# The second normalisation written wholly by GpSimd, with VectorE's part in it taken away

## The chip, the core and the metric

The kernel runs on one core of a Trainium2 chip. A core has TensorE (PE, with its weight loads as PEld), VectorE (DVE), ScalarE (ACT), GpSimd (POOL) and SyncE (SP), each with its own instruction queue, and they meet only through semaphores. The metric is the device time of one launch in microseconds, lower is better.

## What is computed

Sixteen blocks of 128 tokens with 128 features go through gated cross-attention and then through a mixture of nine experts, two chosen per token:

```python
x = x + tanh(g_xattn) * xattn(ctx, layernorm(x), mask, mask, ...)     # 8 heads of 16
x = x + tanh(g_ffn) * ffn(layernorm(x), ...)                          # this layernorm is the second normalisation

def _layernorm(x, axis=-1, eps=1e-05):
    return (x - mean) / sqrt(var + eps)

# ffn: scores = sigmoid(x @ gate.T + bias); top 2 of 9 experts, weights scaled to sum 1
#      out += cw[:, e] * ((silu(x @ w1[e].T) * (x @ w3[e].T)) @ w2[e].T)
```

All arithmetic is float32 except where the experts' first products are split into two float32r parts.

## The kernel before

There are three stages. **Projections**: keys, values, queries and the first half of the output projection, four groups of four blocks. **Attention and routing**: a software pipeline over steps k = 0 to 16 (`turns(step)` on every engine). In step k, PE makes the scores of block k, turns the probabilities of block k-1 and multiplies them with the values, and finishes block k-2 (turn, normalise, output projection). Block k-3 gets its second normalisation: its normalised rows are turned by PE (line 1039) and multiplied with the gate weights (line 1047). **Experts**: token rows that were scattered into a table in DRAM by expert are read back in 40 tiles of 128 rows, go through one expert each, and are scattered to a second table; the last blocks of the attention stage are finished between the first tiles (`between(k)` on each engine). At the end the two results per token are added.

Every engine works through its program in the order written; what sets the order is the code itself, and nothing reorders it. PE's order within a step is: scores, turn of block k-2, turn of the probabilities, `turn_rows` (line 1033 for block k-2, then line 1039 for block k-3, which waits for semaphore `ln2`), the products with the values (line 1001), `gate_and_out` (lines 1047, 1049). So line 1001 stands behind line 1039 in the queue.

The second normalisation of block b, in step b+3: DVE adds the block to x (line 745) and takes mean and variance into `mv2` (lines 747, 751, semaphore `var2`). POOL adds epsilon (line 496) and raises to the power -0.5 (line 498, into `rs2`, semaphore `rstd2`). DVE writes (x - mean) * rs2 into copy 0 of `stage` (line 725, semaphore `ln2`). POOL copies copy 0 to copy 1 (line 490, `keep`, semaphore `kept`), because every token row goes to two experts. POOL then scatters both copies of a group's blocks by indirect DMA (line 508), one group of four blocks some steps later: two of these DMAs in steps 9 and 13, two in steps 10 and 14, four in steps 11 and 15. POOL also prepares the values of each block (lines 475, 477). DVE's order in a step is: maxima of the first four heads (line 706), `unturn` (lines 712, 716), line 725, maxima of the last four heads (line 706), routing work that differs from step to step, and line 745 onwards.

The last two blocks, 14 and 15, are normalised at the start of the expert stage: line 725 for them stands in DVE's `between(0)` and `between(2)`, and PE turns the rows in its own `between(0)` and `between(2)`. POOL does lines 496 and 498 for them among the scatters of group 2, ahead of its first expert tile.

Of the kernel before, what the change touches and what calls it, by code (L numbers as in the profile page):

```python
# [18 lines left out]
ALU = mybir.AluOpType  # L19
# [7 lines left out]
P = 128  # L27
NB = 16
D = 128
# [3 lines left out]
UN = 4  # L33
# [29 lines left out]
def build(nc, x, ctxT, mask, maskT, g2, consts, w_srcT, b_src, w_tgtT, b_tgt, w_outT, b_out,  # L63
          w13T, w2T, gateT, gate_b, x_rows, y_rows, out):
    with ExitStack() as ctx:
# [29 lines left out]
        xs = sb("xs", [P, NB, D])  # L95
# [28 lines left out]
        stage = sb("stage", [P, 2, 2, UN, RW])  # L124
# [80 lines left out]
        def on(k, lag):  # L205

            return 0 <= k - lag < NB
# [224 lines left out]
        def _(pool):  # L432
# [37 lines left out]
            def step(k, r, i):  # L470
# [7 lines left out]
                if on(k, 3):  # L478
                    rstd2_of(k - 3)
# [3 lines left out]
                if on(k, 3):  # L483
                    keep(k - 3)

            def keep(b):

                par, place = b // UN % 2, b % UN
                pool.wait_ge(ln2, b + 1)
                nc.gpsimd.tensor_copy(stage[:, par, 1, place, 0:D], stage[:, par, 0, place, 0:D]).then_inc(kept, 1)  # L490

            def rstd2_of(b):

                q = b % 2
                pool.wait_ge(var2, b + 1)
                nc.gpsimd.tensor_scalar(ve2[:, q:q + 1], mv2[:, q, 1:2], LN_EPS, None, ALU.add).then_inc(eps_added, 1)
                pool.wait_ge(eps_added, b + 1)
                nc.gpsimd.tensor_tensor(rs2[:, q:q + 1], ve2[:, q:q + 1], minus_half[:, 0:1], ALU.pow).then_inc(rstd2, 1)

# [27 lines left out]
            rstd2_of(NB - 2)  # L527
            scatter(NG - 2, 0)
            keep(NB - 2)
            scatter(NG - 2, 1)  # L530
            rstd2_of(NB - 1)
            scatter(NG - 2, 2)
            keep(NB - 1)
# [8 lines left out]
        def _(dve):  # L542
# [176 lines left out]
            def norm2(b):  # L719

                q, par, place = b % 2, b // UN % 2, b % UN
                dve.wait_ge(rstd2, b + 1)
                if b >= 2 * UN:
                    dve.wait_ge(st_rows[place], (b // UN - 1) * 32)
                nc.vector.scalar_tensor_tensor(stage[:, par, 0, place, 0:D], xs[:, b, :], mv2[:, q, 0:1], rs2[:, q:q + 1].to_broadcast([P, D]),
                                               ALU.subtract, ALU.mult).then_inc(ln2, 1)

# [25 lines left out]
            def step(k, r, i):  # L753
# [4 lines left out]
                if on(k, 3):  # L758
                    norm2(k - 3)
# [116 lines left out]
            def between(k):  # L876

                if k == 0:
                    norm2(NB - 2)
                    table_used(0)  # L880
# [3 lines left out]
                if k == 2:  # L884
                    norm2(NB - 1)
                    table_rows(1)
# [318 lines left out]
```

## Time and profile before

| | us |
|---|---|
| median of 3 runs | 243.07 |
| the 3 runs | 243.07, 243.14, 240.57 |
| the profiled execution | 240.22 |
| its span in the trace | 238.4 |
| PE busy | 191.4 (80% of the span) |
| DVE, ACT, POOL busy | 145.1, 143.4, 127.7 |

The profiled execution is a run of its own: its time is 1.8 us above its span, and it lies 2.85 us under the median. The granted TensorE clock was 0.933 of full speed over that execution. Busy shares are means over three stages with different limits, so the stage matters more than the share.

### The profile page before, as it was taken

The page shows a single profiled execution, that of the slowest core. Times are in us where ns is not written, and L with a number is a line of the kernel's source. Part 1 is how long each engine was busy: PE and PEld are TensorE (multiplying, and loading weights), DVE is VectorE, ACT ScalarE, POOL GpSimd, SP SyncE. Part 2 cuts the span into 40 slices and gives each one's busy share as a digit, 9 for nine tenths or more (in the row PEclk, how much of TensorE's full clock was granted, in tenths as well). Part 3 has the DMA queues.
Part 4 walks back from the last instruction along what each step waited for, and adds up shares of the span by engine and source line. Part 5 has one row for each costly group of instructions (what it writes and reads, how often), then busy time and mean ns, then how long its engine had stood idle before and what let it go on. Part 6 is the DMA issues. An engine that isn't in the chain of part 4 may idle for free.

```text
span 238.4 us, 5685 instructions
## 1 busy us (share of the span) xinstructions
PE 191.4 (80%) x1480; PEld 157.7 (66%) x1481; DVE 145.1 (61%) x535; ACT 143.4 (60%) x401; POOL 127.7 (54%) x224
## 2 busy tenths in 40 slices
PE   0099898799997997898677969997999999998200
PEld 0087675457665664666456959997999999998100
DVE  1228788688799779799759447943343344442045
ACT  1525776998796887489433474765666666665100
POOL 4225644524552688468568533678776555555400
PEclk9999999999999999799857788999999999999955
DMA  4994999999900001001122111222321222110087
GB/s 144 344 293 114 311 364 405 404 404 341 303 20 1 26 22 45 3 22 37 36 73 78 48 36 43 76 67 68 94 82 51 61 53 59 44 39 27 0 301 227
DMA packets 21143, 30.78 MB, mean 129 GB/s; under 512 B 3312, under 2 KB 14324, under 8 KB 21120
## 3 DMA queue, kind: packets, MB, share of 16 engines
q1 hardware_dynamic: 17280, 25.74, 32.7%
q0 software_dynamic: 2304, 4.24, 5.4%
q10 hardware_dynamic: 1536, 0.54, 0.9%
q8 instruction: 10, 0.16, 0.3%
q14 instruction: 13, 0.11, 0.1%
HBM read 14.97 MB, written 16.05 MB: 130 GB/s over the span
## 4 chain that ended last, share of the span: by engine, by line
PE 52%; DVE 14%; DMA 11%; issue 7%; POOL 7%; ACT 6%; SPq 2%; POOLq 0%; DVEq 0%; ACTq 0%
PE pt_ps L1117 9%; DMA mask_b<-in_mask 6%; PE score_ps L1084 5%; POOL x_rows L508 4%; PE pt_ps L1126 4%; PE score_ps L1086 4%; PE score_ps L1085 4%; PE score_ps L951 4%; PE score_ps L927 3%; PE ps_a L1001 3%; DMA kheads<-y_rows 3%; DVE less L706 2%; PE score_ps L937 2%; PE pt_ps L989 2%; ACT probs L343 2%
## 5 line engine op out<-in xcount | busy, mean ns | idle before, releaser
L524 POOL DMA_INDIRECT y_rows<-probsT,ids x40 | 39.7, 992 | 26.6 <-ACT probsT L410 21.6
L343 ACT ACTIVATE probs<-score_ps,less 128x128 f32<-128x128 f32 x128 | 37.9, 421 | 0.4 <-DVE less L706 0.4
L508 POOL DMA_INDIRECT x_rows<-stage,slot x32 | 32.4, 1012 | 9.0 <-issue 8.0
L1117 PE MATMUL pt_ps<-w,probsT 128*128 x240 | 34.8, 283 | 1.4 <-ACT probsT L417 1.4
L1117 PEld LDWEIGHTS pt_ps<-w,probsT 128*128 128x128 f32 x240 | 32.7, 197 | 2.2 <-issue 1.9
L860 DVE TENSOR_TENSOR xg_low<-ps_a,xg_high 128x128 fp32r<-128x128 f32 x40 | 11.6, 290 | 34.8 <-ACT xg_high L395 34.6
L410 ACT ACTIVATE probsT<-pt_ps,xg 128x128 f32<-128x128 f32 x40 | 14.7, 367 | 29.7 <-PE pt_ps L1117 29.7
L1084 PE MATMUL score_ps<-w_high,xg_low 128*128 x80 | 30.8, 386 | 0.6 <-issue 0.2
L1086 PE MATMUL score_ps<-w_high,xg_high 128*128 x80 | 26.9, 336 | 0.0
L1085 PE MATMUL score_ps<-w_low,xg_high 128*128 x80 | 26.9, 336 | 0.0
L867 DVE TENSOR_TENSOR probs<-probs,score_ps 128x352 f32<-128x352 f32 x40 | 20.8, 520 | 9.8 <-ACT probs L402 9.0
L706 DVE TENSOR_REDUCE less<-score_ps 128x4 f32<-128x512 f32 x32 | 21.7, 684 | 4.9 <-PE score_ps L958 4.9
L402 ACT ACTIVATE probs<-score_ps 128x352 f32<-128x352 f32 x40 | 18.6, 466 | 4.7 <-PE score_ps L1086 4.2
L1126 PE MATMUL pt_ps<-cst,probs 128*128 128x128 f32 x120 | 20.4, 281 | 0.0
L927 PE MATMUL score_ps<-w_src,ctx_r 128*128 128x128 f32 x64 | 9.7, 314 | 13.2 <-DMA mask_b<-in_mask 13.2
L417 ACT COPY probsT<-pt_ps 128x384 f32<-128x384 f32 x40 | 19.1, 479 | 1.3 <-PE pt_ps L1126 1.3
L951 PE MATMUL score_ps<-kheads,qT 64*128 64x256 f32 x128 | 19.1, 419 | 0.1
L989 PE MATMUL pt_ps<-cst,probs 128*128 128x128 f32 x128 | 16.9, 274 | 1.6 <-ACT probs L343 1.6
L927 PEld LDWEIGHTS score_ps<-w_src,ctx_r 128*128 128x128 f32 x64 | 9.0, 225 | 13.3 <-issue 12.9
L1084 PEld LDWEIGHTS score_ps<-w_high,xg_low 128*128 128x128 f32 x80 | 16.0, 201 | 2.5 <-issue 1.7
L1085 PEld LDWEIGHTS score_ps<-w_low,xg_high 128*128 128x128 f32 x80 | 16.1, 202 | 0.0
L989 PEld LDWEIGHTS pt_ps<-cst,probs 128*128 128x128 f32 x128 | 14.4, 141 | 2.4 <-ACT probs L343 2.3
(150 smaller groups left out, 408.0 us busy)
## 6 DMA issues: line engine op xcount, KB each, us to landing
x_rows<-pads SPq DMA_DIRECT2D x1, 9945.0 KB, 35.4
w_low<-in_w13T SPq DMA_DIRECT2D x3, 1056.0 KB, 8.9
xg<-x_rows SPq DMA_DIRECT2D x40, 65.0 KB, 1.9
ctx_r<-in_ctxT SPq DMA_DIRECT2D x4, 512.0 KB, 6.2
w<-in_w2T SPq DMA_DIRECT2D x1, 1728.0 KB, 12.2
kheads<-y_rows SPq DMA_DIRECT2D x3, 512.0 KB, 5.0
mask_b<-in_mask SPq DMA_DIRECT2D x4, 256.0 KB, 7.3
xs<-in_x SPq DMA_DIRECT2D x3, 256.0 KB, 9.2
```

The lines of the kernel that those rows point to most:

```text
L343: last = nc.scalar.activation(probs[:, r % 2, h, :], score_ps[:, r % 2, h, :], ACT.Exp, bias=less[:, r % 2, h:h + 1])
L508: pool.indirect_dma_start(x_rows[:, :], bass.IndirectOffsetOnAxis(ap=slot[:, par, c, p:p + 1], axis=0), stage[:, par, c, p, :], None, boun ...
L524: pool.indirect_dma_start(y_rows[:, :], bass.IndirectOffsetOnAxis(ap=ids[:, r:r + 1], axis=0), yt[:, r, :], None, bounds_check=last_row, o ...
L706: nc.vector.tensor_reduce(less[:, r % 2, here], score_ps[:, r % 2, here, :], AX.X, ALU.max, negate=True).then_inc(lessened, 1)
L927: last = nc.tensor.matmul(bank[0][:, b * P:(b + 1) * P], ctx_r[:, r, f, b * P:(b + 1) * P], w_src[:, f, D:2 * D], start=(f == 0), stop=(f ...
L951: nc.tensor.matmul(score_ps[:, r % 2, half * HH + 2 * pair:half * HH + 2 * pair + 2, :], qT[rows, k * P:(k + 1) * P], kheads[rows, heads, ...
L989: last = nc.tensor.transpose(pt_ps[:, half, h, :], probs[:, q, half * UN + h, :], ident)
L1084: nc.tensor.matmul(dst[:, 0:HID], xg_low[:, q, :], of(w13_high), start=True, stop=False)
L1085: nc.tensor.matmul(dst[:, 0:HID], xg_high[:, q, :], of(w13_low), start=False, stop=False)
L1086: return nc.tensor.matmul(dst[:, 0:HID], xg_high[:, q, :], of(w13_high), start=False, stop=True)
L1117: last = nc.tensor.matmul(bank[5][:, 0:D], hidT[:, q3, c, :], w2[:, bass.ds(e3, 1), c, :].rearrange("p o d -> p (o d)"), start=(c == 0), s ...
L1126: last = nc.tensor.transpose(bank[4][:, c * P:(c + 1) * P], hid[:, q2, c0:c0 + P], ident)
```

## The change

POOL's `norm2` now does the whole second normalisation: epsilon, power, and then the row (x - mean) * rs2 written twice straight from x into copies 0 and 1 of `stage`, by two `tensor_scalar` instructions with the mean and the power as scalars per partition. The first signals `ln2`, the second `kept`. DVE's line 725 and POOL's copy (line 490) are gone. POOL now waits for its own `rstd2`, and the wait for the scatter that last read the place in `stage` (`st_rows`) moves from DVE to POOL. On POOL both rows are written ahead of the step's scatters; the copy stood behind them.

```diff
--- before.py
+++ after.py
@@ -476,26 +476,23 @@
                                             mask_t[:, bass.ds(k, 1)].unsqueeze(1).to_broadcast([P, H, HD]), ALU.mult)
                     nc.gpsimd.tensor_copy(v_cur[:, r, :, HD:HD + 1], live_t[:, bass.ds(k, 1)].unsqueeze(1).to_broadcast([P, H, 1])).then_inc(v_set, 1)
                 if on(k, 3):
-                    rstd2_of(k - 3)
+                    norm2(k - 3)
                 for p in range(UN):
                     if routed(k, r, 2 * UN + 1 + min(p, 2)) is not None:
                         scatter(routed(k, r, 2 * UN + 1 + min(p, 2)), p)
-                if on(k, 3):
-                    keep(k - 3)
-
-            def keep(b):
-
-                par, place = b // UN % 2, b % UN
-                pool.wait_ge(ln2, b + 1)
-                nc.gpsimd.tensor_copy(stage[:, par, 1, place, 0:D], stage[:, par, 0, place, 0:D]).then_inc(kept, 1)
-
-            def rstd2_of(b):
-
-                q = b % 2
+
+            def norm2(b):
+
+                q, par, place = b % 2, b // UN % 2, b % UN
                 pool.wait_ge(var2, b + 1)
                 nc.gpsimd.tensor_scalar(ve2[:, q:q + 1], mv2[:, q, 1:2], LN_EPS, None, ALU.add).then_inc(eps_added, 1)
                 pool.wait_ge(eps_added, b + 1)
                 nc.gpsimd.tensor_tensor(rs2[:, q:q + 1], ve2[:, q:q + 1], minus_half[:, 0:1], ALU.pow).then_inc(rstd2, 1)
+                pool.wait_ge(rstd2, b + 1)
+                if b >= 2 * UN:
+                    pool.wait_ge(st_rows[place], (b // UN - 1) * 32)
+                for c, done in enumerate((ln2, kept)):
+                    nc.gpsimd.tensor_scalar(stage[:, par, c, place, 0:D], xs[:, b, :], mv2[:, q, 0:1], rs2[:, q:q + 1], ALU.subtract, ALU.mult).then_inc(done, 1)
 
             def scatter(g, p):
 
@@ -524,13 +521,11 @@
                 pool.indirect_dma_start(y_rows[:, :], bass.IndirectOffsetOnAxis(ap=ids[:, r:r + 1], axis=0), yt[:, r, :], None,
                                         bounds_check=last_row, oob_is_err=False).then_inc(st_y[r], 16)
 
-            rstd2_of(NB - 2)
+            norm2(NB - 2)
             scatter(NG - 2, 0)
-            keep(NB - 2)
             scatter(NG - 2, 1)
-            rstd2_of(NB - 1)
+            norm2(NB - 1)
             scatter(NG - 2, 2)
-            keep(NB - 1)
             scatter(NG - 2, 3)
             for k in range(NT):
                 tile(k, k % TR)
@@ -716,15 +711,6 @@
                 nc.vector.tensor_tensor(upd[:, q, :].rearrange("p (h d) -> p h d", h=H), turned[:, :, 0:HD],
                                         rden[:, q, :].unsqueeze(2).to_broadcast([P, H, HD]), ALU.mult).then_inc(normed, 1)
 
-            def norm2(b):
-
-                q, par, place = b % 2, b // UN % 2, b % UN
-                dve.wait_ge(rstd2, b + 1)
-                if b >= 2 * UN:
-                    dve.wait_ge(st_rows[place], (b // UN - 1) * 32)
-                nc.vector.scalar_tensor_tensor(stage[:, par, 0, place, 0:D], xs[:, b, :], mv2[:, q, 0:1], rs2[:, q:q + 1].to_broadcast([P, D]),
-                                               ALU.subtract, ALU.mult).then_inc(ln2, 1)
-
             def logits_of(g):
 
                 dve.wait_ge(lg_mm, g * UN + UN)
@@ -755,8 +741,6 @@
                     maxima(k, r, 0)
                 if on(k, 2):
                     unturn(k - 2, r % 2)
-                if on(k, 3):
-                    norm2(k - 3)
                 if on(k, 0):
                     maxima(k, r, 1)
                 if 2 + k < NE:
@@ -876,13 +860,11 @@
             def between(k):
 
                 if k == 0:
-                    norm2(NB - 2)
                     table_used(0)
                 if k == 1:
                     second(NB - 1)
                     table_counts(1)
                 if k == 2:
-                    norm2(NB - 1)
                     table_rows(1)
                 if k == 3:
                     logits_of(NG - 1)
```

In the order of POOL's instructions, in steps 9 and 10 (`stage` holds the normalised rows, `v_cur` the values of one block, `rs` is the power, `ve` the variance with epsilon), there stood before:

```order
L496 TENSOR_SCALAR ve<-mv 128x1
L498 TENSOR_TENSOR rs<-ve,minus_half 128x1
L508 DMA x_rows<-stage,slot 19712x130 x2
L490 COPY stage<-stage 128x128
L475 TENSOR_TENSOR v_cur<-vals,mask_t 128x8x16
L477 COPY v_cur<-live_t 128x8
L496 TENSOR_SCALAR ve<-mv 128x1
L498 TENSOR_TENSOR rs<-ve,minus_half 128x1
```

And now, in the same steps:

```order
L488 TENSOR_SCALAR ve<-mv 128x1
L490 TENSOR_TENSOR rs<-ve,minus_half 128x1
L495 TENSOR_SCALAR stage<-xs,mv,rs 128x128 x2
L505 DMA x_rows<-stage,slot 19712x130 x2
L475 TENSOR_TENSOR v_cur<-vals,mask_t 128x8x16
L477 COPY v_cur<-live_t 128x8
L488 TENSOR_SCALAR ve<-mv 128x1
L490 TENSOR_TENSOR rs<-ve,minus_half 128x1
```

One instruction behind the scatters has become two ahead of them. In the order of DVE's instructions, in step 13 (`upd` is the attention's output, `less` the negated maxima, `filled` the first instruction of a table for the experts), there stood before:

```order
L706 TENSOR_REDUCE less<-score_ps 128x4
L712 RECIPROCAL rden<-ps_b 128x8
L716 TENSOR_TENSOR upd<-ps_b,rden 128x128
L725 SCALAR_TENSOR_TENSOR stage<-xs,mv,rs 128x128
L706 TENSOR_REDUCE less<-score_ps 128x4
L806 TENSOR_TENSOR filled<-next_row,cst 1x144
```

And now, in the same step:

```order
L701 TENSOR_REDUCE less<-score_ps 128x4
L707 RECIPROCAL rden<-ps_b 128x8
L711 TENSOR_TENSOR upd<-ps_b,rden 128x128
L701 TENSOR_REDUCE less<-score_ps 128x4
L790 TENSOR_TENSOR filled<-next_row,cst 1x144
```

DVE goes from `upd` straight to the second maxima. PE's, ACT's and SP's instructions are the same in both kernels, in the same order.

## Rows read from the trace of the kernel before

**Rows 1.** The page: the chain that ended last, shares of the span by engine
```profile
PE 52%; DVE 14%; DMA 11%; issue 7%; POOL 7%; ACT 6%; SPq 2%; POOLq 0%; DVEq 0%; ACTq 0%
```

**Rows 2.** Stretches: length, busy PE, PEld, DVE, ACT, POOL; PE clock; DMA share; GB/s
```profile
44.00:68.00 24.00, 23.07 (x231) 15.47 (x231) 17.93 (x45) 21.40 (x71) 10.14 (x23) 1.00 0.92 326
68.00:98.00 30.00, 25.65 (x266) 18.01 (x262) 25.53 (x111) 22.36 (x74) 17.86 (x38) 0.99 0.06 20
```

**Rows 3.** Groups by line: busy us, mean ns; then idle before
```profile
L475 POOL TENSOR_TENSOR v_cur<-vals,mask_t 128x128 f32<-128x128 f32 x16 | 7.2, 450 | 0.0
L490 POOL COPY stage<-stage 128x128 f32<-128x128 f32 x16 | 4.8, 302 | 7.5 <-DVE stage L725 7.5
L725 DVE SCALAR_TENSOR_TENSOR stage<-xs,mv,rs 128x128 f32<-128x128 f32 x16 | 5.5, 344 | 0.4 <-POOL rs L498 0.4
```

**Rows 4.** Timeline of DVE in step 11: start us, us, instruction
```profile
89.31 0.34 DVE L725 SCALAR_TENSOR_TENSOR stage<-xs,mv,rs 128x128 f32<-128x128 f32 x1
89.57 0.68 DVE L706 TENSOR_REDUCE less<-score_ps 128x4 f32<-128x512 f32 x1
```

**Rows 5.** Timeline of POOL, steps 9 to 12
```profile
79.04 0.57 POOL L498 TENSOR_TENSOR rs<-ve,minus_half 128x1 f32<-128x1 f32 x1
79.94 1.23 POOL L508 DMA_INDIRECT x_rows<-stage,slot  x1 [0.33 <-DVE slot L700]
...
83.54 0.23 POOL L496 TENSOR_SCALAR ve<-mv 128x1 f32<-128x1 f32 x1 [0.30 <-DVE mv L751]
...
87.95 0.24 POOL L496 TENSOR_SCALAR ve<-mv 128x1 f32<-128x1 f32 x1 [0.16 <-DVE mv L751]
88.27 0.57 POOL L498 TENSOR_TENSOR rs<-ve,minus_half 128x1 f32<-128x1 f32 x1
89.03 1.10 POOL L508 DMA_INDIRECT x_rows<-stage,slot  x1 [0.19 <-issue]
...
93.95 0.30 POOL L490 COPY stage<-stage 128x128 f32<-128x128 f32 x1
94.21 0.41 POOL L475 TENSOR_TENSOR v_cur<-vals,mask_t 128x128 f32<-128x128 f32 x1
...
95.08 0.57 POOL L498 TENSOR_TENSOR rs<-ve,minus_half 128x1 f32<-128x1 f32 x1
```

**Rows 6.** Timeline of PE in step 12
```profile
96.36 0.27 PE L1039 MATMUL ps_b<-cst,stage 128*128 128x128 f32 x1
```

**Rows 7.** The chain that ended last, steps 13 to 16: start us, us, what
```profile
101.83 0.34 DVE stage L725
...
105.66 0.57 POOL rs L498
...
116.25 0.58 POOL rs L498
...
116.85 0.36 DVE stage L725
...
117.26 0.33 PE ps_b L1039
```

**Rows 8.** Timeline, blocks 14 and 15 at the start of the experts
```profile
121.01 0.57 POOL L498 TENSOR_TENSOR rs<-ve,minus_half 128x1 f32<-128x1 f32 x1
121.89 1.11 POOL L508 DMA_INDIRECT x_rows<-stage,slot  x1 [0.31 <-DVE slot L700]
...
127.03 0.25 POOL L496 TENSOR_SCALAR ve<-mv 128x1 f32<-128x1 f32 x1
127.36 0.57 POOL L498 TENSOR_TENSOR rs<-ve,minus_half 128x1 f32<-128x1 f32 x1
129.45 0.33 PE L1039 MATMUL ps_b<-cst,stage 128*128 128x128 f32 x1 [1.09 <-DVE stage L725]
```

**Rows 9.** POOL's line 477 in step 3, and DVE beside it
```profile
53.29 0.86 POOL L477 COPY v_cur<-live_t 128x8 f32<-128x8 f32 x1
53.15 0.94 DVE L583 TENSOR_TENSOR w_low<-w_low,w_high 128x704 fp32r<-128x704 f32 x1
```

## The prediction

> **What bounds the kernel now.** I first read the chain that ended last, for who sets the end: PE 52%, DVE 14%, POOL 7% [rows 1]. Then the busy time by stretch, because the change only touches the attention steps and the first expert tiles. From 44 to 68 us (steps 2 to 6, no scatters) ACT is busy 21.40 of 24.00 us and POOL 10.14: these steps are ACT's and PE's, and POOL has room. From 68 to 98 us (steps 7 to 11) DVE is busy 25.53 of 30.00 and POOL 17.86, the scatters having begun [rows 2]. Last I read the timelines of POOL and PE, for how much room stands between the end of POOL's power and the moment PE turns the rows. The reader is to see three things. After a power in a late step POOL goes straight on: at 88.84 it ends, and the scatter starts at 89.03 [rows 5]. Late in step 11's four scatters POOL is behind: the power of block 9 ends at 95.65, PE's line 1039 starts at 96.36, and PE has line 1001 queued behind it [rows 5, 6]. And in steps 14 to 16 the chain itself runs through POOL: power at 105.66, scatters from 106.42, power at 116.25, DVE's line 725 at 116.85, PE at 117.26 [rows 7].
>
> **What DVE loses.** Sixteen instructions of 0.344 us [rows 3]. Line 725 starts at 89.31 and the next at 89.57, so each holds the queue for 0.26 us [rows 4], 16 x 0.26 = 4.2 us in all. In the ACT-bound steps, blocks 0 to 3, that is worth nothing: ACT's work hides it, and if ACT were faster it would be worth at most 0.26 us a step. It is on the path where DVE ends the step: step 7 (block 4), step 11 (block 8) and step 13 (block 10, on the chain at 101.83 [rows 7]). Step 11's gain is spent again, because step 12 waits for POOL; I count steps 7 and 13, **-0.26 x 2 = -0.52 us**.
>
> **What POOL gets.** It loses the copy, 0.302 us long [rows 3], from 93.95 to the next start at 94.21, so 0.26 of the queue [rows 5]. It gets two instructions that read 128x128, subtract a scalar and multiply by another. No row shows this form; call its duration d. The lower end is the copy of the same size, 0.30. The upper end is two passes with two operands each, as line 475 is (0.41 at 94.21 [rows 5]): 0.76 when the second follows within 0.05 of the first's end. I take **d = 0.40**: one streamed operand like the copy, but two scalars to fetch and two operations, so close to line 475 and its mean of 0.45 [rows 3]. A pair costs more than 2d by little: POOL waits for its own power, which costs 0.08 (the epsilon ends at 88.19, the power starts at 88.27 [rows 5]), and the second overlaps the first by 0.05. So each pair puts 2d + 0.03 = 0.83 us ahead of the step's scatters and takes 0.26 away behind them. PE's wait changes too: it was power, DVE's line, PE; it is power, 0.08, d, and 0.05 to signal PE.
>
> The Trainium skill bears on d. By its page GPSIMD Engine Reference (section 4.1, Engine selection) elementwise work with two inputs is about twice as slow on GpSimd, with one input roughly line-rate, and the page advises VectorE for it. Twice line 725 would be about 0.69; the trace here has a one-input copy at 0.302, under DVE's 0.344, which speaks for the one-input half of that rule. By the two-input half the sum below would be about +5.4 instead of +1.1.
>
> **Steps 9 to 12.** The first scatter could start at 79.04 + 0.57 + 0.19 = 79.80 and starts at 79.94, for the slots: 0.14 of room [rows 5]. Three pairs go ahead of scatters (blocks 6, 7, 8), three copies go. POOL idled 0.30 before the epsilon at 83.54 and 0.16 before the one at 87.95 [rows 5]; this room is filled first. So the power of block 9 ends 3 x 0.83 - 3 x 0.26 - 0.14 - 0.46 = 1.11 later than 95.65. PE then starts line 1039 at 96.76 + 0.08 + 0.40 + 0.05 = 97.29 instead of 96.36: **+0.93 us**, in d it is 7d - 1.87. Line 1001, the value products and the next scores stand behind it, so all of it counts.
>
> **Steps 14 to 16.** POOL has no idle left once `var2` of block 11 has come. Pairs for blocks 11 and 12, less two copies: 2 x 0.57 = 1.14. For block 13 the power ended at 116.83 and PE started at 117.26, 0.43 later [rows 7]; now 0.53. That is 1.14 + 0.10 = **+1.24 us**, or 5d - 0.76. The same POOL delay moves the scatters of group 1; their readers, the first expert tiles, start after 120 us and have that room.
>
> **Blocks 14 and 15, among the tiles.** The scatter at 121.89 had 0.12 of room behind a power that ended at 121.58 (0.19 of the 0.31 being the usual gap) [rows 8]. Pair in, copy out: epsilon and power of block 15 come 0.83 - 0.12 - 0.26 = 0.45 later, so the power ends at 128.38. But DVE's line 725 stood behind an expert tile's multiply there, and PE waited until 129.45, 1.09 of it idle [rows 8]. Now PE can start at 128.38 + 0.53 = 128.91: **-0.54 us**, 3d - 1.74. If d were small this gain would end at the 1.09.
>
> What else moves costs nothing: steps 3 to 8 have no scatter beside POOL's pairs, and POOL's 10.14 of 24 us leaves the room [rows 2]; the wait for `st_rows` that POOL takes over looks at scatters issued at least two steps earlier on the same queue; group 2's scatters end about 1 us later, ahead of tiles that PE reaches only some ten us afterwards, where POOL waits for the tiles anyway.
>
> **The sum**: -0.52 + 0.93 + 1.24 - 0.54 = **+1.1 us**, in d it is 15d - 4.9. Its ends are -0.4 (d = 0.30) and +6.5 (d = 0.76). Against the profiled execution's 240.22 that is 241.3. The median lies 2.85 above that execution, and two of three runs lie at 243.1, so I forecast the median at 243.07 + 1.1 = **244.2 us**.
>
> **The rivals.**
> 1. *The rows are dear on POOL.* Same mechanism, other side of the bound: 1% is 2.4 us (about what a measurement of this kernel can tell from no change, its own runs lying 1.1% apart), and 15d - 4.9 reaches it at d = 0.49. At 0.55 the time is 243.07 + 3.3 = 246.4. For it: scalars from memory, and 0.23 to 0.25 for an epsilon of one element per partition, which a copy of 128 undercuts per element by far [rows 5, 8]. Against it: the copy's 0.302 [rows 3]. Chance 0.27.
> 2. *POOL and DVE block each other over memory reads.* The 8-element copy at 53.29 took 0.86 us beside DVE's long two-operand line 583 from 53.15 [rows 9]. POOL now reads 32 x 128 elements where it read 16. If each pair of the ten blocks 6 to 15 met one such block of 0.2 us (an estimate between nothing and the 0.86), that is another +2.0, 246.2 in all. Against it: line 583 ends with step 6, and DVE's line 725, itself a reader of two operands from that memory, is gone; the instructions that now stand there read PSUM. By the Trainium skill, SBUF — State Buffer (section Who interferes with whom), a DVE instruction with two SBUF inputs and a GpSimd one that reads SBUF exclude each other; the row at 53.29 agrees, with 0.86. A falling TensorE clock, as PE waits longer in steps 12 and 16, works the same way. Chance 0.14.
> 3. *The relief of DVE decides.* If POOL's lag were covered, as it would be were the steps DVE's throughout, the 16 x 0.26 = 4.2 us would be gained: 238.9. Against it: ACT's 21.40 of 24.00 in five steps [rows 2], and the chain on POOL after 105 us. Chance 0.08.
>
> That the change does not do what it says is excluded by the order of instructions. My forecast's own mechanism, with d between 0.30 and 0.49, has 0.51. Faster by over 1%: 0.08; within 1%: 0.51; slower: 0.27 + 0.14 = 0.41. The range: low, the forecast's low end of -0.4 and up to 1.7 less, because the median may fall toward the lower of the runs shown, 241.0; high, d = 0.60 with +4.1, 247.2.
>
> **What would show it.** In the changed kernel, the two new POOL instructions at 0.40 each (0.30 to 0.49), with starts 0.35 apart. DVE's second maxima starting right behind `upd`. PE's line 1039 of step 12 waiting for POOL by about 1 us more than before, and the chain going from POOL's rows straight to PE in step 16. The gap before line 1039 in the tiles (1.09) smaller by half. It is wrong if the new form costs over 0.5, if DVE's instructions get longer beside it, if the mean granted clock moves far from 0.933, or if PE's wait in steps 12 and 16 does not grow.

## The result: 4% slower, and outside the range

The changed kernel takes 251.01 us (median of 4 runs, 246.95 to 254.05) against 241.82 for the kernel before (4 runs, 239.09 to 243.14). The ratio is 1.040, with a 95% interval of 1.027 to 1.053. The forecast was 244.2, range 241.0 to 247.2, with "within 1%" likelier than "slower". The direction was the forecast's, the size was not. Where a ratio with an interval is given, here and below, it compares only each kernel's faster runs, since most of the others show a lower granted clock; medians are over all runs. The profiled execution took 250.45 us with a span of 248.6, against 240.22 and 238.4 before.

The page of the changed kernel, first the shares of the chain that ended last and then the group of the new instruction (busy us, mean ns, idle before it):

```profile
PE 43%; POOL 22%; DMA 10%; DVE 9%; issue 8%; ACT 5%; SPq 2%; POOLq 0%; DVEq 0%; ACTq 0%
L495 POOL TENSOR_SCALAR stage<-xs,mv,rs 128x128 f32<-128x128 f32 x32 | 25.5, 801 | 1.7
```

POOL's share of the chain went from 7% [rows 1] to 22%. The new instruction takes 0.801 us, where the sum had 0.40 and its upper bound 0.76.

POOL's timeline in the steps of [rows 5] (L490 is now the power, L488 the epsilon, L505 the scatter; x2 is the pair of rows):

```profile
79.77 0.57 POOL L490 TENSOR_TENSOR rs<-ve,minus_half 128x1 f32<-128x1 f32 x1
80.44 1.58 POOL L495 TENSOR_SCALAR stage<-xs,mv,rs 128x128 f32<-128x128 f32 x2
82.22 1.23 POOL L505 DMA_INDIRECT x_rows<-stage,slot  x1 [0.20 <-issue]
...
90.95 0.25 POOL L488 TENSOR_SCALAR ve<-mv 128x1 f32<-128x1 f32 x1
91.29 0.57 POOL L490 TENSOR_TENSOR rs<-ve,minus_half 128x1 f32<-128x1 f32 x1
91.97 1.61 POOL L495 TENSOR_SCALAR stage<-xs,mv,rs 128x128 f32<-128x128 f32 x2
93.75 1.10 POOL L505 DMA_INDIRECT x_rows<-stage,slot  x1 [0.18 <-POOL stage L495]
...
99.54 0.57 POOL L490 TENSOR_TENSOR rs<-ve,minus_half 128x1 f32<-128x1 f32 x1
100.22 1.59 POOL L495 TENSOR_SCALAR stage<-xs,mv,rs 128x128 f32<-128x128 f32 x2
```

The power of block 9 starts at 99.54 instead of 95.08. The two lie on time axes whose block 0 differs by 0.6 us, so 3.8 of the 4.5 us are delay. The idle 0.30 and 0.16 us ahead of the epsilons of blocks 7 and 8 are gone: POOL waits for no other engine from 79.77 to 102. PE's lines that answer to [rows 6] and [rows 8], blocks 7, 8, 9, 12, 13 and 15:

```profile
87.15 0.33 PE L1021 MATMUL ps_b<-cst,stage 128*128 128x128 f32 x1 [1.16 <-POOL stage L495]
92.83 0.33 PE L1021 MATMUL ps_b<-cst,stage 128*128 128x128 f32 x1 [1.25 <-POOL stage L495]
101.08 0.48 PE L1021 MATMUL ps_b<-cst,stage 128*128 128x128 f32 x1 [2.40 <-POOL stage L495]
118.53 0.33 PE L1021 MATMUL ps_b<-cst,stage 128*128 128x128 f32 x1 [1.33 <-POOL stage L495]
126.28 0.48 PE L1021 MATMUL ps_b<-cst,stage 128*128 128x128 f32 x1 [2.32 <-POOL stage L495]
139.58 0.33 PE L1021 MATMUL ps_b<-cst,stage 128*128 128x128 f32 x1 [1.64 <-POOL stage L495]
```

These starts are the ruler for all that follows: each block's rows are turned once, and PE's work stands behind that turn. The columns are the time between such starts, in the profiled execution of each kernel; the rows below the second are the experiments.

| kernel | block 0 at | 0 to 6 | 6 to 9 | 9 to 10 | 10 to 13 | 13 to 15 | 0 to 15 | 15 to end of span |
|---|---|---|---|---|---|---|---|---|
| before | 52.69 | 28.28 | 15.39 | 5.86 | 15.04 | 12.19 | 76.76 | 108.95 |
| changed | 53.31 | 28.36 | 19.41 | 6.83 | 18.37 | 13.30 | 86.27 | 109.02 |
| changed, second time | 52.67 | 29.14 | 18.80 | 6.82 | 18.35 | 13.30 | 86.41 | 107.22 |
| forms (attention steps as changed) | 53.40 | 28.38 | 19.46 | 7.14 | 18.22 | 13.34 | 86.54 | (longer program) |
| copy_rows | 55.15 | 28.38 | 15.82 | 7.15 | 15.43 | 10.57 | 77.35 | 108.90 |
| second_row | 52.13 | 28.23 | 16.35 | 7.15 | 16.11 | 11.91 | 79.75 | 106.62 |
| one_row | 52.26 | 28.35 | 17.78 | 5.64 | 17.24 | 12.84 | 81.85 | 107.29 |
| handoff | 52.41 | 28.35 | 19.27 | 7.20 | 17.81 | 12.80 | 85.43 | 107.16 |
| one_wide | 53.13 | 30.23 | 18.78 | 6.57 | 17.98 | 13.34 | 86.90 | 108.87 |
| warm | 52.72 | 29.10 | 18.78 | 4.77 | 18.87 | 12.20 | 83.72 | 109.46 |
| dve_both | 52.45 | 30.66 | 15.61 | 5.09 | 15.67 | 11.39 | 78.42 | 111.33 |
| warm_before | 53.48 | 28.28 | 15.44 | 4.80 | 15.11 | 11.44 | 75.07 | 107.45 |
| warm_before, last chip | 53.17 | 28.27 | 16.28 | 4.80 | 18.18 | 11.58 | 79.11 | 116.52 |
| warm_dve, last chip | 53.00 | 28.83 | 16.61 | 5.09 | 16.43 | 11.01 | 77.97 | 119.33 |

Of the span's 10.2 us, 4.0 came between blocks 6 and 9, 1.0 from 9 to 10, 3.3 from 10 to 13, 1.1 from 13 to 15, and 0.8 elsewhere, of which 0.6 was there already at block 0. The last column differs by several us between kernels with the same expert stage. Over about the first 30 us of it the mean granted clock was 1.00 in second_row (106.62), 0.89 in before (108.95) and 0.84 in warm (109.46). The column says nothing about the change.

The experiments ran on four chips in turn: copy_rows, second_row, one_row and handoff on the first; forms, the change again, warm and dve_both on the second; warm_before and one_wide on the third; warm_before again and warm_dve on the last. The kernel before ran beside them each time, and a median is compared only with the one from the same chip.

### The profile page after: what moved, and what is told of

Same layout as the page of the kernel before. It is cut to its first block, busy times and chain, and to the rows that moved or that the text cites. A ratio compares the mean times of both kernels' runs of the same rounds, so it can differ in the third digit from the quotient of the medians.

```text
span 248.6 us, 5685 instructions
## 1 busy us (share of the span) xinstructions
PE 194.1 (78%) x1480; PEld 159.7 (64%) x1481; DVE 140.3 (56%) x519; ACT 144.0 (58%) x401; POOL 147.3 (59%) x240
## 4 chain that ended last, share of the span: by engine, by line
PE 43%; POOL 22%; DMA 10%; DVE 9%; issue 8%; ACT 5%; SPq 2%; POOLq 0%; DVEq 0%; ACTq 0%
POOL x_rows L505 9%; PE pt_ps L1099 9%; POOL stage L495 6%; DMA mask_b<-in_mask 6%; PE score_ps L1066 5%; PE pt_ps L1108 4%; PE score_ps L1068 4%; PE score_ps L1067 4%; POOL rs L490 3%; PE score_ps L909 3%; PE ps_a L983 3%; DVE xs L895 2%; PE score_ps L919 2%; ACT probs L343 2%; DMA kheads<-y_rows 2%
## 5 line engine op out<-in xcount | busy, mean ns | idle before, releaser
L505 POOL DMA_INDIRECT x_rows<-stage,slot x32 | 32.2, 1008 | 8.7 <-issue 8.0
L495 POOL TENSOR_SCALAR stage<-xs,mv,rs 128x128 f32<-128x128 f32 x32 | 25.5, 801 | 1.7
L1108 PE MATMUL pt_ps<-cst,probs 128*128 128x128 f32 x120 | 20.7, 284 | 0.0
L971 PE MATMUL pt_ps<-cst,probs 128*128 128x128 f32 x128 | 18.1, 287 | 1.6 <-ACT probs L343 1.6
L971 PEld LDWEIGHTS pt_ps<-cst,probs 128*128 128x128 f32 x128 | 15.4, 148 | 2.6 <-ACT probs L343 2.5
```

Of the source, the lines that this page charges most:

```text
L495: nc.gpsimd.tensor_scalar(stage[:, par, c, place, 0:D], xs[:, b, :], mv2[:, q, 0:1], rs2[:, q:q + 1], ALU.subtract, ALU.mult).then_inc(don ...
L505: pool.indirect_dma_start(x_rows[:, :], bass.IndirectOffsetOnAxis(ap=slot[:, par, c, p:p + 1], axis=0), stage[:, par, c, p, :], None, boun ...
L971: last = nc.tensor.transpose(pt_ps[:, half, h, :], probs[:, q, half * UN + h, :], ident)
L1108: last = nc.tensor.transpose(bank[4][:, c * P:(c + 1) * P], hid[:, q2, c0:c0 + P], ident)
```

## The experiments

### What the new instruction costs, and what in it

```diff
+                    if form == "copy":
+                        last = nc.gpsimd.tensor_copy(dst, src)
...
+                    if form == "ptr2":
+                        last = nc.gpsimd.tensor_scalar(dst, src, s0, s1, ALU.subtract, ALU.mult)
...
+                    n += 1
+                    last.then_inc(ten, 1)
+                    pool.wait_ge(ten, n)
```

> The changed kernel with eleven extra GpSimd instructions at the end of its program, twice over, each waiting for the one in front: copy, tensor_scalar with one and two constants, with one and two scalars per partition, tensor_tensor with a broadcast second operand, all 128x128; then two scalars at widths 8, 64 and 256, two constants at 8 and 256. What makes 0.80 us: if fetching the scalars, then two constants take about 0.4 and the time of two scalars at width 8 is about 0.6; if the second operation, one constant is about 0.4 and two 0.8; if the tensor_scalar body at any number of operations, all four are about 0.8 and the slope from width 8 to 256 is near 4.5 ns per element, against 0.84 for the copy.

The whole kernel took 263.28 us (one run); only the durations at its end count. POOL's timeline there: L544 copy, L546 one constant, L548 two constants, L550 one scalar per partition, L552 two scalars per partition, L554 tensor_tensor with a broadcast second operand:

```profile
237.60 0.29 POOL L544 COPY v_cur<-cst 128x128 f32<-128x128 f32 x1 [1.56 <-DMA y_rows<-probsT,ids]
237.99 0.55 POOL L546 TENSOR_SCALAR v_cur<-cst 128x128 f32<-128x128 f32 x1
238.62 0.65 POOL L548 TENSOR_SCALAR v_cur<-cst 128x128 f32<-128x128 f32 x1
239.37 0.61 POOL L550 TENSOR_SCALAR v_cur<-cst,minus_half 128x128 f32<-128x128 f32 x1
240.09 0.81 POOL L552 TENSOR_SCALAR v_cur<-cst,minus_half,minus_one 128x128 f32<-128x128 f32 x1
240.97 0.40 POOL L554 TENSOR_TENSOR v_cur<-cst,minus_half 128x128 f32<-128x128 f32 x1
```

Other widths, from the second round, when DVE and the DMA queues had finished:

```profile
251.16 0.41 POOL L552 TENSOR_SCALAR v_cur<-cst,minus_half,minus_one 128x8 f32<-128x8 f32 x1
252.35 1.22 POOL L552 TENSOR_SCALAR v_cur<-cst,minus_half,minus_one 128x256 f32<-128x256 f32 x1
253.66 0.26 POOL L548 TENSOR_SCALAR v_cur<-cst 128x8 f32<-128x8 f32 x1
254.00 1.07 POOL L548 TENSOR_SCALAR v_cur<-cst 128x256 f32<-128x256 f32 x1
```

The instruction costs 0.81 us by itself, in the second round with nothing beside it, so 0.801 in the kernel needs no contention. None of the three causes expected is the whole one. At width 128 the form is dear from the start, 0.55 with a single constant against 0.29 for a copy; a second operation adds 0.10 (0.55 to 0.65); a scalar from memory in place of a constant adds 0.06 (0.55 to 0.61), and two of them 0.16 (0.65 to 0.81). Over the widths the two lines run side by side: two scalars cost 0.15 to 0.16 us more than two constants at 8, at 128 and at 256 elements, and both grow by 3.2 to 3.3 ns per element. By these numbers (an estimate) 0.42 of the 0.81 is the price of 128 elements and 0.15 that of the two scalars. A copy grew only from 0.20 at 8 elements (line 477) to 0.29 at 128, 0.8 ns per element. And a tensor_tensor of the same size, its second operand broadcast, takes 0.40, half as long: what looks like the two-input instruction is the cheap one here.

In the first round the narrow and wide forms ran beside DVE's closing additions, which read two operands from memory, and beside busy DMA engines, and took longer: 0.94 instead of 0.41 at width 8 with two scalars, 1.45 instead of 1.07 at 256 with two constants. So they can be held up; which of the two neighbours did it is not separated here.

### Queue time or the handing over

Five kernels change POOL's queue time per block in steps of their own. Theory A is always that time on POOL's queue sets the loss; theory B is the rival named in each expectation. The medians of the first four rest on 4 runs each, 4 to 6 us apart, and the lowest runs lie further from before's lowest (236.21 us) than the medians do: by 4.0 us in copy_rows, 4.1 in second_row, 7.0 in one_row, 10.6 in handoff. So the argument goes by the stretches of the traces. In the terms of the prediction each block in a late step adds Q us net to POOL's queue, and the way from power to PE takes p instead of 0.43. Then blocks 6 to 9 grow by 3Q - 0.60 + p - 0.71 (0.60 is the room of 0.14 and 0.46), and 10 to 13 by 2Q + p - 0.43.

**copy_rows**: the two instructions become plain copies of x; the normalisation of the row is left out.

```diff
-                    nc.gpsimd.tensor_scalar(stage[:, par, c, place, 0:D], xs[:, b, :], mv2[:, q, 0:1], rs2[:, q:q + 1], ALU.subtract, ALU.mult).then_inc(done, 1)
+                    nc.gpsimd.tensor_copy(stage[:, par, c, place, 0:D], xs[:, b, :]).then_inc(done, 1)
```

> The changed kernel with its two tensor_scalar instructions replaced by two plain copies of x: the row is not normalised, everything else (order, signals, waits, DVE's relief) is the change's. Theory A (the whole loss is the duration d of the new instruction on POOL's queue, times the places where POOL is late): at the copy's 0.30 us the formula 15d - 4.9 gives -0.4, so within 1% of before, and PE's wait before the turned rows in steps 10, 11, 12, 15 and 16 (1.2, 1.2, 2.4, 1.3, 2.3 us) shrinks to under 0.6. Theory B (handing the rows from POOL to PE, or the moved waits, cost by themselves): 3 us or more over before whatever d is.

Measured: 242.66 us (4 runs, 240.21 to 243.97), before beside it 240.63 (7 runs, 236.21 to 242.46). Two us over by the medians, of expected -0.4 or over +3. From block 0 to block 15 it takes 0.6 us longer than before, where the change takes 9.5. The new group's row:

```profile
L495 POOL COPY stage<-xs 128x128 f32<-128x128 f32 x32 | 8.4, 294 | 1.0
```

The two late stretches grew by 0.43 and 0.39, so order, waits and handing over are nearly free there and theory B falls; the step from block 9 to 10 took 1.3 us more, which is taken up below. PE's wait ahead of the turned rows was gone in steps 10, 11 and 15, but 1.00 and 1.02 us were left in steps 12 and 16, where I had expected under 0.6.

**second_row**: the kernel before with only its copy replaced.

```diff
-                nc.gpsimd.tensor_copy(stage[:, par, 1, place, 0:D], stage[:, par, 0, place, 0:D]).then_inc(kept, 1)
+                nc.gpsimd.tensor_scalar(stage[:, par, 1, place, 0:D], xs[:, b, :], mv2[:, b % 2, 0:1], rs2[:, b % 2:b % 2 + 1], ALU.subtract, ALU.mult).then_inc(kept, 1)
```

> The kernel before with one edit: the plain copy behind the scatters is replaced by the tensor_scalar straight from x (copy 1 of the row). DVE and PE's release as before. Theory A: 0.5 us more per block on POOL's queue at the three late places: 0.6 + 1.0 + 0.4 = +2.0 us, though PE never waits for this instruction's result. Theory B: no change, since nothing on the path reads it.

Measured: 244.30 us (4 runs, 240.34 to 246.20) against 240.63, +3.7, of expected +2.0 or nothing; from block 0 to 15 it is +3.0. Nothing on PE's way reads this instruction, and yet PE's turns come 1.0 and 1.1 us later in the two stretches. It delays what stands behind it in the queue.

**one_row**: the change with its first instruction, and the plain copy behind the scatters.

```diff
-                for c, done in enumerate((ln2, kept)):
-                    nc.gpsimd.tensor_scalar(stage[:, par, c, place, 0:D], xs[:, b, :], mv2[:, q, 0:1], rs2[:, q:q + 1], ALU.subtract, ALU.mult).then_inc(done, 1)
+                nc.gpsimd.tensor_scalar(stage[:, par, 0, place, 0:D], xs[:, b, :], mv2[:, q, 0:1], rs2[:, q:q + 1], ALU.subtract, ALU.mult).then_inc(ln2, 1)
...
+                if on(k, 3):
+                    keep(k - 3)
```

> The changed kernel with only copy 0 written by tensor_scalar ahead of the scatters, and copy 1 by the plain copy behind them, as before the change. Theory A: net queue time per block 0.88 us instead of 1.37, the three late places then give -0.5 + 2.3 + 2.3 + 0.2 = +4.2 us over before, between before and the change. Theory B (what costs is the first instruction, on the way to PE, alone): as slow as the change, +9.

Measured: 245.66 us (4 runs, 243.22 to 249.35) against 240.63, +5.0 of expected +4.2, not +9; from block 0 to 15 it is +5.1.

**handoff**: POOL's queue as in the change, PE released by DVE as before (the lines added last stand in DVE's step).

```diff
-                for c, done in enumerate((ln2, kept)):
-                    nc.gpsimd.tensor_scalar(stage[:, par, c, place, 0:D], xs[:, b, :], mv2[:, q, 0:1], rs2[:, q:q + 1], ALU.subtract, ALU.mult).then_inc(done, 1)
+                for to, done in ((scr[:, :], scratched), (stage[:, par, 1, place, 0:D], kept)):
+                    nc.gpsimd.tensor_scalar(to, xs[:, b, :], mv2[:, q, 0:1], rs2[:, q:q + 1], ALU.subtract, ALU.mult).then_inc(done, 1)
...
+                if on(k, 3):
+                    norm2(k - 3)
```

> POOL's program as in the change, instruction for instruction, but its first tensor_scalar writes a scratch tile, and DVE writes copy 0 and releases PE, at its old place. So POOL's queue is as loaded as in the change, and PE waits for DVE. Theory A (queue time): +6.1 us over before, 1.0 to 1.5 less than the formula's 7.1 for the change. Theory B (the loss is PE waiting on POOL's row and not on DVE's): under +2.5.

Measured: 248.10 us (4 runs, 246.78 to 251.09) against 240.63, +7.5 of expected +6.1; from block 0 to 15 it is +8.7. PE's turn of block 9 in this kernel:

```profile
100.03 0.33 PE L1036 MATMUL ps_b<-cst,stage 128*128 128x128 f32 x1 [2.24 <-DVE stage L722]
```

The wait is 2.24 us and is put down to DVE. DVE was not the cause: it had waited 2.41 us for POOL's power (line 492) itself. Most of the change's loss is here although PE waits for DVE again, so theory B falls a second time.

POOL's queue is not quite as loaded as in the change. Its first instruction of each pair, which starts together with DVE's line 722 in the late steps, took longer than the second:

```profile
L497 POOL TENSOR_SCALAR scr<-xs,mv,rs 128x128 f32<-128x128 f32 x16 | 14.0, 877 | 1.7
```

It took 0.96 us for blocks 7 and 8, when line 722 ran beside it, and 0.81 for block 6, when it did not; the second of the pair took 0.79 on average.

**one_wide**: both copies by one instruction of twice the width.

```diff
-                for c, done in enumerate((ln2, kept)):
-                    nc.gpsimd.tensor_scalar(stage[:, par, c, place, 0:D], xs[:, b, :], mv2[:, q, 0:1], rs2[:, q:q + 1], ALU.subtract, ALU.mult).then_inc(done, 1)
+                nc.gpsimd.tensor_scalar(stage[:, par, :, place, 0:D], xs[:, b:b + 1, :].to_broadcast([P, 2, D]), mv2[:, q, 0:1], rs2[:, q:q + 1], ALU.subtract, ALU.mult).then_inc(ln2, 1)
```

> The changed kernel with its two tensor_scalar instructions made one that reads the row twice and writes both copies (256 elements per partition). By the forms measured alone it takes about 1.22 us instead of 2 x 0.80. Theory A (time on POOL's queue): 1.07 net per block instead of 1.37, but PE waits for the whole of it, so +3.3 in steps 9 to 12, +3.1 in 14 to 16, +0.8 in the tiles, less 0.5: +6.7 over before by the terms, half a us under the change. Theory B (number of elements sets the price, not the number of instructions): as the change or slower, +9.

Measured: 251.17 us (4 runs, 250.72 to 251.42) against 240.34, ratio 1.050 (1.042 to 1.058): +10.8, of expected +6.7 by theory A and +9 by theory B. The scatters wait for `ln2` in place of `kept`. The instruction took about what it took alone (1.22), and not twice 0.80, so theory B's reason is not there:

```profile
L494 POOL TENSOR_SCALAR stage<-xs,mv,rs 128x256 f32<-128x256 f32 x16 | 19.9, 1243 | 1.7
```

The two stretches are as theory A has them, but the total is not, and it is as slow as the change. The table shows where theory A was blind: blocks 0 to 6 took 30.23 instead of 28.28. With 1.24 us to wait for, PE is held in the early steps too (0.46 to 0.57 us ahead of the turned rows of blocks 0 to 4), which I had costed at nothing for every version.

The formula against the table, growth over before in us:

| kernel | Q, p | 6 to 9: formula, trace | 10 to 13: formula, trace |
|---|---|---|---|
| copy_rows | 0.37, 0.43 | 0.23, 0.43 | 0.74, 0.39 |
| second_row | 0.50, 0.43 | 0.62, 0.96 | 1.00, 1.07 |
| one_row | 0.88, 0.93 | 2.26, 2.39 | 2.26, 2.20 |
| one_wide | 1.07, 1.38 | 3.28, 3.39 | 3.09, 2.94 |
| handoff | 1.37, 0.43 | 3.23, 3.88 | 2.74, 2.77 |
| changed (and again) | 1.37, 0.93 | 3.73, 4.02 (3.41) | 3.24, 3.33 (3.31) |

Six kernels, one formula, and the trace is within 0.35 us of it in all but one place (handoff, 0.65, of which the longer instructions of blocks 6 to 8 are about 0.4). That POOL's queue time at the places where POOL is late sets these two stretches is shown.

### TensorE's clock behind the longer waits

**warm**: the change with PE's idle filled. **after_again** is the change once more, on the same chip.

```diff
+                    for _ in range({10: 6, 11: 6, 12: 16, 15: 6, 16: 16}.get(k, 0)):
+                        nc.tensor.transpose(ps_b[:, 2 * P:3 * P], ident, ident)
                     pe.wait_ge(ln2, b + 1)
```

> The changed kernel with idle PE filled: 6 extra turns of the identity ahead of the turned rows in steps 10, 11 and 15, 16 in steps 12 and 16, into a part of PSUM that is free there; about 0.7 and 1.8 us of work inside waits of 1.2 to 2.4 us. Theory C (part of the loss is the TensorE clock that falls after long idle, about 1.2 us in step 13 and some in the first tiles): 1 to 3 us less than the change, with the granted clock from 98 to 122 us near before's 0.86 or above, instead of 0.84. Theory A alone: the same time as the change.

> The change once more, for comparison with the kernels of this call: ratio 1.03 to 1.05 over before.

Measured: warm 246.98 us (4 runs, 245.55 to 248.62), ratio to before 1.026 (1.014 to 1.037); the change again 251.66 (6 runs), ratio 1.047 (1.038 to 1.057). That is 4.7 us less for fifty more turns, and more than the 1 to 3 expected. Of it the profiled executions show 2.7 us between blocks 0 and 15 (83.72 for 86.41); after block 15 warm's was 2.2 us the slower, with PE idle 2.83 us ahead of block 15's turn, so that their spans differ by only 0.4. Where the rest of the 4.7 lies is not shown. The step from block 9 to block 10, a stretch of each kernel: length, busy PE, PEld, DVE, ACT, POOL, granted clock. First before, then warm; of the change the row begins at 101 us:

```profile
96.40:102.20 5.80, 5.80 (x43) 3.81 (x41) 4.56 (x21) 3.27 (x12) 2.78 (x7) 0.71 0.01 3
```

```profile
100.60:105.40 4.80, 4.27 (x43) 3.10 (x43) 3.01 (x14) 3.79 (x12) 3.21 (x7) 1.00 0.00 0
```

```profile
101.00:108.00 7.00, 6.92 (x43) 4.90 (x43) 3.56 (x15) 3.10 (x11) 4.14 (x9) 0.55 0.01 2
```

The same 43 PE records take 5.8 us at a mean granted clock of 0.71, 4.8 at 1.00, and 7.0 (the step itself 6.8) at 0.55. Full clock is 2.4 GHz; at 0.55 most of the step ran at the lower level of 1.2. Ahead of these steps PE had idled 2.23 us for DVE in the kernel before; 1.27 for DVE and then 2.40 for POOL in the change; in warm 1.27 for DVE, then it had turned the identity 16 times (98.04 to 99.95) and idled 0.65. Theory C is shown for this step: 2.05 us between the change and warm (6.82 to 4.77).

The length of a wait alone does not tell the level. First before, then dve_both (a kernel of the next section):

```profile
96.00 0.19 PE L1011 MATMUL ps_b<-both,rows_below 128*128 128x36 bf16 x1 [2.23 <-DVE upd L716]
```

```profile
98.36 0.19 PE L1001 MATMUL ps_b<-both,rows_below 128*128 128x36 bf16 x1 [2.18 <-DVE upd L706]
```

The waits are alike, but the step behind ran at 0.71 in before and at 1.00 in dve_both (5.09 us). In copy_rows the waits were only 1.54 and 1.00, and the step ran at 0.52. What decides between them is not shown by these runs.

From 98 to 122 us the mean clock was 0.84 in the change, 0.86 when repeated, 1.00 in warm. It is 0.86 in the kernel before as well, so the clock is a loss that the kernel had. The change made it larger: 0.55 for 0.71 in this step, and from 122 to 140 us, over the last blocks, 0.55 for 0.74.

**warm_before**: the same idea in the kernel before, and a second time on another chip.

```diff
+                for _ in range({8: 14, 12: 16, 16: 10}.get(k, 0)):
+                    nc.tensor.transpose(ps_a[:, 0:P], ident, ident)
                 if on(k, 2):
                     pe.wait_ge(normed, k - 1)
```

> The kernel before with idle PE filled: 14, 16 and 10 extra turns of the identity ahead of the turn of the attention's output in steps 8, 12 and 16, where PE waits 1.5, 2.2 and 1.4 us for DVE; the target is a part of PSUM that is free then. About 0.11 us each, so 1.5, 1.8 and 1.1 us, inside the waits. Theory C (idle PE makes the clock fall, and what follows at the lower clock is paid for): step 13 (from the turned rows of block 9 to those of block 10) takes 4.8 to 5.1 us instead of 5.86, and the time is 1 to 2 us under before. Rival: the clock's level has no part in the time of these steps, same time, or slower by what the extra turns stick out.

> The kernel before with the 14, 16 and 10 extra turns in PE's waits of steps 8, 12 and 16, once more. If what it saved in step 13 (5.86 to 4.80 us) carries to the end: median again 1 to 2 us under before's. If the first difference was spread between runs: no difference.

Measured, third chip: 238.51 us (12 runs, 237.26 to 241.58) against 240.34 (17 runs, 235.94 to 243.76). The ratio is 1.002 (0.997 to 1.008). The step from block 9 to 10 took 4.80, as expected. Last chip: 251.54 (12 runs) against 253.28 (24 runs), ratio 0.999 (0.993 to 1.004); the step again took 4.80. Both medians are 1.8 us lower (1.80 and 1.74), and both intervals hold 1. The saving in that step is shown in both profiled executions; that the kernel is faster is not.

On the last chip every kernel was about 13 us slower, the one before too. In warm_before's profile there, 8.1 us of it is one wait of PE, put down to nothing that the profile shows (who waited for whom, total, times, longest):

```profile
PE pt_ps L1119 <- issue: 8.1, 1, 8.1
```

ScalarE and DVE stood still at the same place, between 155 and 165 us, for 5.99 and 5.09 us. warm_dve's profile on that chip has the same stop (PE 10.3 us, ScalarE 6.0, DVE 7.9), and no profile on the other chips has it, so it belongs to that chip or that time and not to one kernel. Its cause is open, and times of that chip are compared only with each other.

### DVE for both copies

**dve_both**: the opposite move; the lines taken out last are POOL's copy. **warm_dve** adds the extra turns of warm_before.

```diff
-                nc.vector.scalar_tensor_tensor(stage[:, par, 0, place, 0:D], xs[:, b, :], mv2[:, q, 0:1], rs2[:, q:q + 1].to_broadcast([P, D]),
-                                               ALU.subtract, ALU.mult).then_inc(ln2, 1)
+                for c, done in enumerate((ln2, kept)):
+                    nc.vector.tensor_scalar(stage[:, par, c, place, 0:D], xs[:, b, :], mv2[:, q, 0:1], rs2[:, q:q + 1], ALU.subtract, ALU.mult).then_inc(done, 1)
...
-                if on(k, 3):
-                    keep(k - 3)
```

> The other way round: DVE writes both copies by two tensor_scalar instructions at its old place and POOL's copy is gone, from the kernel before. By the queue argument POOL gains 0.26 us per block at the late places (2 x 0.26 in steps 14 to 16, 1 to 3 x 0.26 in steps 9 to 12), DVE loses about 0.2 us a step where it ends the step (7, 11, 13): -0.5 us in all, the same within 1%. If DVE's time counted as much as POOL's, +1 or more.

> DVE writes both copies and POOL's copy is gone, plus the same extra turns of PE in steps 8, 12 and 16. DVE writing both measured 1.3% over before, with the lower clock from step 8 on (its turned rows of block 6 came 2.4 us later). If that loss was the clock: now within 1% of before, 1 to 2 us under it at best. If DVE's two instructions cost by their own time: still 1% or more over, near 243.5.

Measured: dve_both 244.04 us (4 runs), ratio 1.013 (1.003 to 1.024), where I expected no change and priced +1 or more for the rival that DVE's time counts as much as POOL's. DVE's instruction is 0.351 us long, 0.45 less than the same one on POOL:

```profile
L716 DVE TENSOR_SCALAR stage<-xs,mv,rs 128x128 f32<-128x128 f32 x32 | 9.7, 351 | 0.0
```

Its span is 3.8 us longer than before's, and 2.4 of it stand between blocks 0 and 6: PE waited 1.89 us for DVE in step 8, 1.50 before, and the next stretch ran at half clock:

```profile
78.30:83.10 4.80, 4.80 (x22) 3.71 (x22) 4.00 (x16) 1.65 (x6) 2.96 (x4) 0.50 0.05 16
```

Another 2.4 us stand after block 15 (111.33 for 108.95), at about the same granted clock in the first 30 us (0.89); what they come from is not shown.

warm_dve: 252.85 us (12 runs) against 253.28, ratio 1.007 (1.003 to 1.011), and 1.3 us over warm_before's 251.54 on the same chip. Its step from block 5 to 6 ran at a granted clock of 1.00 and took 4.95 us, where dve_both's took 6.78 at 0.55, and blocks 0 to 6 took 28.83. So of dve_both's 2.4 us there, 1.8 go with the clock and about 0.5 are left, which fits DVE's own time in the steps that it ends. No version tried beats the kernel before beyond doubt.

## Why the prediction was wrong

**The step that failed is "I take d = 0.40".** The instruction took 0.801 us. The prediction's own sum, 15d - 4.9, gives +7.1 at that value, so this one number accounts for 6.0 of the 9.1 us between its +1.1 and the span's +10.2. The bounds failed as well, "two passes with two operands each", 0.76: they took a two-operand instruction as the dearest, and it is the cheapest of the forms measured that compute (0.40). I took the new form as "one streamed operand like the copy". A copy does not compute; the nearest row by form was the epsilon, a tensor_scalar, and its 0.23 to 0.25 at one element against about 0.20 for small copies (line 477) hid the cost per element, which is 3.2 to 3.3 ns in the form with two operations. The row to distrust was the neighbour in size but not in form.

The other 3.1 us of the 9.1 are 1.2 in the step from block 9 to 10 (1.0 lost instead of 0.26 gained), 0.3 between blocks 0 and 6, where the other 0.26 was to be gained, 0.8 by which the three late stretches overran their formulas, and 0.7 outside the sum, of which 0.6 stood before block 0. With d = 0.80 the forecast would have read 250.2, close to the measured 251.01, but in part by luck: its start value of 243.07 was high, the median before is 241.82 with the fourth run, and between the medians lie +9.2 us.

**The rule that I weighed down.** The Trainium skill's GPSIMD Engine Reference (section 4.1, Engine selection) gives elementwise work with two inputs about twice VectorE's time and with one input roughly line-rate. I let the copy decide for the second half. Measured, the one-input tensor_scalar is 0.801 against 0.351 on DVE, 2.3 times, and the tensor_tensor, its second input broadcast, 0.40. The page's general advice against this change was right, its division into one and two inputs was not, for this form. The sentence in the prediction that put twice line 725 into the sum had +5.4, nearer than my forecast.

**Steps 9 to 12** were to cost 7d - 1.87; at 0.80 that is 3.73, the traces have 4.0 and 3.4. **Steps 14 to 16**, 5d - 0.76 = 3.24, have 3.3 twice. **Blocks 14 and 15**, 3d - 1.74, were forecast as a gain of 0.54 and turn at d = 0.58 into a loss: 0.66 by the formula, 1.1 in the trace. The mechanism on POOL's queue, its places and its terms were right but for the price, and the five variants bear them out.

**Rival 1** was this case, with 0.27; it priced itself at 246.4 for d = 0.55. **Rival 2**, blocking over memory, had no part in the instruction's time: it is 0.81 alone, and in the kernel its 32 executions lie between 0.783 and 0.837. Blocking itself is real, as handoff shows with 0.96 beside DVE's line 722; the change has taken that line away. In steps 3 to 6 the instruction that takes longer was line 477 before (0.86 us, 0.20 in the later steps) and is line 475 now (0.68, 0.39 in the later steps), but there POOL has room. **Rival 3**, DVE's relief, is refuted by copy_rows, which has all of it and a cheap POOL and still is not faster (0.6 us more from block 0 to 15).

**DVE's relief of 0.52** did not appear. Step 7 gained 0.13 (5.79 for 5.92 between the turns of blocks 4 and 5: 71.09 to 76.88, 70.25 to 76.17). Step 13, where 0.26 was to be gained, lost 1.0: **the clock was the term that the sum did not have**. Nor is the relief there at equal clock: at 1.00 the step took 4.80 us in warm_before, with DVE's line, and 4.77 in warm, without it. I named a falling clock as a thing that works like rival 2, and gave it no number, though the clock line of before's page was there to read. Its 40 slices are of 6 us each, in tenths of full speed; the first low ones are slice 17, from 95 us, where step 12 waits and step 13 follows, and 20 to 25, from 113 us, with steps 15 and 16 and the first tiles:

```profile
PEclk9999999999999999799857788999999999999955
```

**"What else moves costs nothing"** held for steps 3 to 8 only roughly: the step took 4.44 instead of 4.37 us (57.75 to 62.19, 57.06 to 61.43), as PE now gets the row a little later in each: in handoff, where DVE writes it, the step is 4.37 again. With one_wide it is 4.86.

Of the signs that I asked for, DVE's order and POOL's way to PE came as said; the waits ahead of the turned rows in steps 12 and 16 grew by more than the 1 us named (from nothing to 2.40, from 0.21 to 2.32), and the gap ahead of block 15's turn grew to 1.64 where it was to halve from 1.09.

## What to carry to other kernels

A queue that is ahead on average can be the limit in a few steps; count an added instruction once for every step from the last idle moment to the wait that it delays, and price it there. Price an instruction by a row of its own form: size and number of operands misled here by a factor of two (0.40 for 0.801), and where no such row exists the range must say so. When a change lengthens waits of TensorE, read the granted clock of the steps behind them, and price those steps at the lower level too: here 1.0 us in one step. The wait's length alone did not tell which level came.

## What the runs showed of the hardware

- GpSimd's tensor_scalar, 128x128 float32, at the end of forms: 0.55 to 0.59 us with one constant, 0.65 with two, 0.61 with one scalar per partition, 0.81 with two; tensor_tensor with a broadcast operand 0.40, copy 0.29. With two operations it grew by 3.2 to 3.3 ns per element between widths 8 and 256, and two scalars cost 0.15 us more than two constants. VectorE's with two scalars: 0.351 (dve_both).
- GpSimd's tensor_scalar took 0.96 us instead of 0.80 when DVE's scalar_tensor_tensor on the same block ran beside it (handoff).
- A step of 43 PE records took 4.8, 5.8 and 7.0 us at mean granted clocks of 1.00, 0.71 and 0.55. Where the identity was turned into free PSUM during the wait ahead of it, the step ran at 1.00 (warm, and warm_before on both chips). One kernel without such turns ran it at 1.00 too, behind a wait of 2.18 us (dve_both).
- A wait put down to DVE (2.24 us in handoff) had its cause in POOL: DVE itself was waiting for POOL's power.
